# Cross-attention decoder layer: keys and values of all heads first, and projections as seven block products

## The chip, the cores and the metric

The kernel runs on one NeuronCore of a Trainium2 chip. A core has TensorE (PE: matmuls; its weight loads are listed as PEld), VectorE (DVE), ScalarE (ACT), GpSimd (POOL), SyncE (SP, which only issues DMAs here) and 16 DMA engines. The metric is device time of one execution in microseconds (us), lower is better. A time is the median of several runs.

## The reference

```python
x = x + attn(layernorm(x))                 # one head of 128, x is (8 batches, 128 tokens, 512), f32
x = x + xattn(layernorm(x), ctx, mask)     # 32 heads of 128, nearly all of the work
x = x + ffn(layernorm(x))                  # 512x512 base, plus top-2 of 8 low-rank experts

# xattn
xn = rmsnorm(h, ln_weight)
h_q, h_k, h_v = xn @ w_q.T, ctx @ w_k.T, ctx @ w_v.T        # each 1024 tokens x 4096
score = softmax(where(m, q k^T + position_bias, -inf))      # per batch and head, 128x128
out = h + (score @ v) @ w_out.T
```

Every f32 product of the projections is made of three fp32r passes: the operands are split in a high part (rounded to fp32r) and a low part (the rest), and hi*hi + hi*lo + lo*hi is accumulated. Scores and the weighing of values are plain f32 matmuls.

## The kernel before

**Tiling.** The 1024 tokens (8 batches of 128) are columns: `xt` (normalised x) and `ct` (context) are 512 features as 4 chunks `c` of 128 partitions x 1024 tokens, each as hi and lo. The 32 heads come in 16 groups of two (`PAIR`). Weights of a group arrive from DRAM as four pieces of 128x1024 (512 KB): QKA, QKB (query and key weights of head 0 and 1), WV, WO. ScalarE makes the high part (`split_weights`, L725), VectorE the low part from two SBUF tensors (`w_lo`, L1000).

**One group on PE**, in its order: `project_qk(g, 0)`, transpose of the last head's probabilities, scores of head 0, weighing of values, `project_v(g)`, transposes, `project_out(g - 1)`, `project_qk(g, 1)`, weighing, scores. `project_qk` makes, per head, two tensors (q and k) x two halves of 512 tokens x 4 chunks x 3 passes = 48 matmuls with 512 columns. `project_v` makes, per batch, 4 x 3 matmuls with 256 columns (both heads), 96 in a group. `project_out` makes, per batch, 2 heads x 3 passes with 512 columns, 48 in a group. PE is the engine whose order the others follow; every wait is written by hand, with semaphores.

**Around it.** VectorE adds bias and mask to the scores out of PSUM (`take_scores`, L960), takes maxima (L967), and after ScalarE's exponentials (L707) scales the probabilities by 1/sum (L973, `row_scale` L977, `probs` L981), splits outputs, and adds each batch's output product from PSUM to `acc` (`add_out`, L878). GpSimd does only `bias_mask` (L337, one 128x1024 addition a head) in the loop, and the low parts of `ct` at the start (L324) and of the FFN's weights at the end (L344). SyncE loads weights and bias.

**Start and end.** Ahead of the loop stand the one-head attention with its layernorms and group 0; the loop runs over groups 1 to 14, group 15 and the last output projection follow by hand, then the FFN. Group 1 begins at 96.2 us, and groups follow at 53.2 us.

Of the kernel before, what the change touches and what calls it, by code (L numbers as in the profile page):

```python
# [20 lines left out]
BANK = 512  # L35
NE, NR = 8, 16
ROUTED = 256
QKV_COLS, OUT_COLS = slice(0, KC * 3 * P), slice(KC * 3 * P, KC * 3 * P + C)
PIECE = PAIR * C
QKA, WV, WO, QKB = range(4)  # L40
# [5 lines left out]

def decoder_kernel(nc, x, ctx_t, mask, w_qkv, b_qkv, w_o, b_o, ln_w, pos_bias, weights, w_base, w_routed, w_lora_b,
                   out):
    with ExitStack() as ctx:
        def sb(name, shape, dt=F32):  # L50
            return ctx.enter_context(nc.sbuf_tensor(name, shape, dt))
# [3 lines left out]


        acc = sb("acc", [P, B, C])
        rows = sb("rows", [P, B, C])
        xt = [sb("xt_hi", [P, KC, T], F32R), sb("xt_lo", [P, KC, T], F32R)]
        ct = [sb("ct_hi", [P, KC, T], F32R), sb("ct_lo", [P, KC, T], F32R)]  # L60
        raw = sb("raw", [P, 4, PIECE])
        w = [sb("w_hi", [P, 4, PIECE], F32R), sb("w_lo", [P, 4, PIECE], F32R)]
        raw_a = sb("raw_a", [P, KC * 3 * P + C])

        ot = [sb("ot_hi", [P, PAIR * T], F32R), sb("ot_lo", [P, PAIR * T], F32R)]
        qt = sb("qt", [P, T])
        kt = sb("kt", [P, T])
        v = sb("v", [P, B, PAIR * P])
        probs = sb("probs", [P, B, P])
        probs_t = sb("probs_t", [P, B, P])  # L70
        bias = sb("bias", [P, PAIR, P])
        bias_mask = sb("bias_mask", [P, B, P])
        mask_add = sb("mask_add", [P, B, P])
        mask_raw = sb("mask_raw", [P, B, P], mask.dtype)
        has_key = sb("has_key", [P, B])
        b_o_rows = bias_mask[:, 0:C // P, :].rearrange("p b n -> p (b n)")
        b_qkv_cols = sb("b_qkv_cols", [P, 3])
        ln_w_cols = sb("ln_w_cols", [P, KC])
        ident = sb("ident", [P, P])
# [11 lines left out]
        neg_max = sb("neg_max", [P, B])  # L91
        sums = sb("sums", [P, B])
        inv = sb("inv", [P, B])
        row_scale = sb("row_scale", [P, B])
        logits = sb("logits", [P, B, NE])
        gates = sb("gates", [P, B, NE])

        beats, ties = (probs_t[:, n:n + 2, :].rearrange("p b (e j) -> p (b e) j", j=NE) for n in (0, 2))
# [5 lines left out]
        ot_last = [t[:, 0:PAIR, :].rearrange("p c n -> p (c n)") for t in xt]  # L104
        WO_LAST = QKA
        w_qkv_s = [t[:, QKV_COLS].rearrange("p (c n) -> p c n", c=KC) for t in ot]
        w_o_s = [t[:, OUT_COLS] for t in ot]
        vt_a = v[:, :, :].rearrange("p b n -> p (b n)")[:, 0:T]
        vt_tiles = v[:, :, :].rearrange("p b n -> p (b n)")[:, T:2 * T]
        ffn_cols = KC * C + KC * ROUTED + C  # L110
        ffn_raw = rows[:, :, :].rearrange("p b n -> p (b n)")[:, 0:ffn_cols]
        ffn = [t[:, :, :].rearrange("p c n -> p (c n)") for t in ct]
# [4 lines left out]

        bank = [ctx.enter_context(nc.psum_tensor(f"bank{i}", [P, BANK], F32)) for i in range(8)]
        QK, SC, TO, VO = bank[0:2], bank[2:4], bank[4:6], bank[6:8]
        ROWS_T = (SC + TO, SC + TO, TO + QK)  # L120
        OWN_OUT = (SC + QK) * 2
# [3 lines left out]

        x_loaded = [sem(f"x_loaded{b}") for b in range(B)]
        raw_loaded = [sem(f"raw_loaded{p}") for p in range(4)]
        raw_qkv_loaded = sem("raw_qkv_loaded")
        raw_o_loaded = sem("raw_o_loaded")
        small_loaded = sem("small_loaded")  # L130
        mask_loaded = sem("mask_loaded")
        bias_loaded = sem("bias_loaded")
        ffn_loaded = sem("ffn_loaded")
        stored = sem("stored")

        ident_ready = sem("ident_ready")
# [70 lines left out]
        def spans(layer, i):  # L207


            return 2 * layer + i + 2  # L210
# [140 lines left out]
        def _(pe):  # L351
# [148 lines left out]
            def last_out():  # L500
# [21 lines left out]
                for b in range(B):  # L522
# [6 lines left out]
                    if b >= 3:  # L529
                        part(b, 0)  # L530
# [752 lines left out]
```

## Time and profile before

| | us |
|---|---|
| median of 3 runs (965.95 to 966.62) | 966.17 |
| span of the profiled execution | 964.8 |
| PE busy | 937.4 (97%) |
| VectorE busy | 470.6 (49%) |
| ScalarE busy | 376.0 (39%) |
| GpSimd busy | 105.9 (11%) |
| DMA queue, share of 16 engines | 14.3% |

The profile shows one execution. A timeline row gives start, length and count of merged instructions; matmuls overlap, so what one costs is read from the distance of starts, not from its length. The chain of waits follows the last instruction back to what released it. PEclk is the granted TensorE clock as a share of 2.4 GHz.

### The profile page before, as it was taken

The page shows a single profiled execution, that of the slowest core. Times are in us where ns is not written, and L with a number is a line of the kernel's source. Part 1 is how long each engine was busy: PE and PEld are TensorE (multiplying, and loading weights), DVE is VectorE, ACT ScalarE, POOL GpSimd, SP SyncE. Part 2 cuts the span into 40 slices and gives each one's busy share as a digit, 9 for nine tenths or more (in the row PEclk, how much of TensorE's full clock was granted, in tenths as well). Part 3 has the DMA queues.
Part 4 walks back from the last instruction along what each step waited for, and adds up shares of the span by engine and source line. Part 5 has one row for each costly group of instructions (what it writes and reads, how often), then busy time and mean ns, then how long its engine had stood idle before and what let it go on. Part 6 is the DMA issues. An engine that isn't in the chain of part 4 may idle for free.

```text
span 964.8 us, 14659 instructions
## 1 busy us (share of the span) xinstructions
PE 937.4 (97%) x5584; PEld 831.5 (86%) x5584; DVE 470.6 (49%) x802; ACT 376.0 (39%) x999; POOL 105.9 (11%) x60
## 2 busy tenths in 40 slices
PE   4899999999999999999999999999999999999798
PEld 4788989889898989898898989898988989898587
DVE  7787545434444435444344444354443444444764
ACT  3555524343443515243434425252434344254030
POOL 3211101010000001010000000010100000000300
PEclk9999999999999999999999999999999999999899
DMA  6402120110111110101101111101011010200002
GB/s 239 131 1 72 50 66 27 42 45 27 46 47 43 32 61 27 65 27 32 55 27 43 49 43 29 64 27 65 24 28 62 27 43 27 98 1 1 0 1 88
DMA packets 15712, 45.45 MB, mean 47 GB/s; under 512 B 2000, under 2 KB 4176, under 8 KB 15568
## 3 DMA queue, kind: packets, MB, share of 16 engines
q1 hardware_dynamic: 15696, 45.23, 14.3%
q8 instruction: 11, 0.18, 0.1%
q14 instruction: 5, 0.04, 0.0%
HBM read 43.13 MB, written 2.10 MB: 47 GB/s over the span
## 4 chain that ended last, share of the span: by engine, by line
PE 93%; DVE 5%; DMA 1%; ACT 0%; POOL 0%; issue 0%; SPq 0%; DVEq 0%
PE bank L358 77%; PE bank L411 6%; PE bank L393 6%; PE bank L401 3%; DVE row_scale L977 1%; DVE rows L916 1%; DMA raw_a<-in_w_qkv 1%; PE bank L376 1%; DVE stats L886 0%; DVE acc L878 0%; DVE acc L1066 0%; DVE xt_lo L948 0%; DVE xt_lo L951 0%; DVE acc L1219 0%; POOL rstd L304 0%; ACT xt_hi L690 0%
## 5 line engine op out<-in xcount | busy, mean ns | idle before, releaser
L337 POOL TENSOR_TENSOR bias_mask<-mask_add,bias 128x1024 f32<-128x1024 f32 x32 | 76.7, 2395 | 713.2 <-DVE probs L960 702.7
L358 PE MATMUL bank<-w_hi,ct_hi 128*128 128x256 f32 x512 | 146.4, 286 | 0.0
L358 PE MATMUL bank<-w_hi,ct_lo 128*128 128x256 f32 x512 | 145.0, 283 | 0.0
L358 PE MATMUL bank<-w_lo,ct_hi 128*128 128x256 f32 x512 | 145.0, 283 | 0.0
L878 DVE TENSOR_TENSOR acc<-bank,acc 128x512 f32<-128x512 f32 x136 | 93.4, 691 | 78.6 <-PE bank L358 78.4
L725 ACT CAST w_hi<-raw 128x1024 fp32r<-128x1024 f32 x64 | 67.3, 1051 | 137.7 <-PE bank L358 137.7
L707 ACT ACTIVATE probs<-probs,neg_max 128x128 f32<-128x128 f32 x264 | 102.8, 393 | 43.1 <-DVE neg_max L967 43.1
L993 DVE TENSOR_TENSOR ot_lo<-bank,ot_hi 128x512 fp32r<-128x512 f32 x62 | 41.7, 689 | 136.8 <-ACT ot_hi L719 136.8
L1000 DVE TENSOR_TENSOR w_lo<-raw,w_hi 128x1024 fp32r<-128x1024 f32 x64 | 79.5, 1260 | 52.6 <-ACT w_hi L725 52.6
L358 PE MATMUL bank<-w_hi,ot_hi 128*128 128x512 f32 x240 | 95.8, 399 | 7.2 <-DVE acc L878 7.2
L358 PE MATMUL bank<-xt_hi,w_hi 128*128 128x512 f32 x256 | 101.6, 397 | 0.9 <-DVE xt_lo L948 0.7
L358 PE MATMUL bank<-ct_hi,w_hi 128*128 128x512 f32 x256 | 99.9, 390 | 0.4 <-DVE w_lo L1000 0.4
L358 PE MATMUL bank<-xt_lo,w_hi 128*128 128x512 f32 x256 | 99.8, 390 | 0.0
L358 PE MATMUL bank<-xt_hi,w_lo 128*128 128x512 f32 x256 | 99.8, 390 | 0.0
L358 PE MATMUL bank<-ct_hi,w_lo 128*128 128x512 f32 x256 | 99.8, 390 | 0.0
L358 PE MATMUL bank<-ct_lo,w_hi 128*128 128x512 f32 x256 | 99.7, 389 | 0.0
L358 PEld LDWEIGHTS bank<-w_hi,ct_hi 128*128 128x128 f32 x512 | 98.3, 192 | 0.3 <-ACT v L735 0.2
L358 PEld LDWEIGHTS bank<-w_lo,ct_hi 128*128 128x128 f32 x512 | 98.3, 192 | 0.1
L358 PEld LDWEIGHTS bank<-w_hi,ct_lo 128*128 128x128 f32 x512 | 98.2, 192 | 0.0
L358 PE MATMUL bank<-w_hi,ot_lo 128*128 128x512 f32 x240 | 94.2, 392 | 0.0
L358 PE MATMUL bank<-w_lo,ot_hi 128*128 128x512 f32 x240 | 94.0, 392 | 0.0
L731 ACT COPY kt<-bank 128x512 f32<-128x512 f32 x64 | 37.5, 586 | 118.8 <-PE bank L358 118.6
(133 smaller groups left out, 1505.0 us busy)
## 6 DMA issues: line engine op xcount, KB each, us to landing
raw<-in_weights SPq DMA_DIRECT2D x64, 512.0 KB, 3.5
acc<-in_x SPq DMA_DIRECT2D x8, 256.0 KB, 6.0
raw<-in_ctx_t SPq DMA_DIRECT2D x4, 512.0 KB, 8.2
bias<-in_pos_bias SPq DMA_DIRECT2D x16, 128.0 KB, 2.0
out_rows<-acc SPq DMA_DIRECT2D x8, 256.0 KB, 2.1
rows<-in_w_base SPq DMA_DIRECT2D x1, 1024.0 KB, 5.6
raw_a<-in_w_qkv SPq DMA_DIRECT2D x1, 768.0 KB, 6.9
rows<-in_w_routed SPq DMA_DIRECT2D x1, 512.0 KB, 6.4
```

Of the source, the lines that this page charges most:

```text
L337: pool.tensor_tensor(bias_mask[:, :, :], mask_add[:, :, :], bias[:, j, :].unsqueeze(1).to_broadcast([P, B, P]), ALU.add).then_inc(bias_mas ...
L358: ins = pe.matmul(out_ap, lhs[a], rhs[b], start=start and k == 0, stop=stop and k == n - 1)
L376: ins = pe.transpose(ROWS_T[layer][c][:, cols(t)], rows[:, HALF * i + t, cols(c)], ident[:, :])
L393: ins = pe.matmul(SC[i][:, cols(t)], qt[:, cols(b)], kt[:, cols(b)], start=True, stop=True)
L401: ins = pe.transpose(TO[i][:, cols(t)], probs[:, HALF * i + t, :], ident[:, :])
L411: ins = pe.matmul(TO[i][:, cols(t)], values(b), probs_t[:, b, :], start=True, stop=True)
L707: ins = act.activation(probs[:, b, :], probs[:, b, :], ACT.Exp, bias=neg_max[:, b:b + 1], accum_out=sums[:, b:b + 1])
L725: act.copy(w[0][:, piece if to is None else to, :], raw[:, piece, :]).then_inc(w_hi_ready[piece], 1)
L731: act.copy((qt, kt)[k // 2][:, cols(k % 2, BANK)], QK[k % 2][:, :]).then_inc(qk_copied, 1)
L878: dve.tensor_tensor(acc[:, b, :], of[:, :], acc[:, b, :], ALU.add).then_inc(out_added, 1)
L993: dve.tensor_tensor(to[1][:, c], TO[i][:, :], to[0][:, c].bitcast(F32), ALU.subtract).then_inc(ot_lo_ready, 1)
L1000: dve.tensor_tensor(w[1][:, to, :], raw[:, piece, :], w[0][:, to, :].bitcast(F32), ALU.subtract).then_inc(w_lo_ready[piece], 1)
```

## The change

1. **Two phases.** First keys and values of all 16 pairs of heads are projected and stored in DRAM (`keys`, `values`, 1 MB each a pair); then, pair by pair, queries are projected, keys and values loaded again, and attention and the output projection done. Everything of `project_qk`, `project_v` and the group order goes.
2. **Seven block products.** Each projection of a pair (two heads x 1024 tokens, 512 features) is seen as 2x2 blocks (heads x feature halves times feature halves x token halves) and made by the Strassen-Winograd scheme: 7 products (`project`, slots 0 to 6) of 2 chunks x 3 passes = 6 matmuls with 512 columns, 42 instead of 48. All run in two PSUM banks that accumulate in turn; ScalarE copies four partial results out (`take`), VectorE adds three.
3. **Sums of blocks.** For the weights, GpSimd makes four 128x256 sums (`sum_weights`), ScalarE four high parts (one of 256 and three of 512 columns), VectorE four low parts (`low`), for each of the three projections of a pair. Context and x get 4 sums, 7 high and 7 low parts of 128x1024, once: for the context on GpSimd, for x on VectorE, between pairs 1 and 3.
4. **Values.** They come out feature-major. VectorE transposes them in 32x32 blocks (`turn_blocks`, 4 operations of 128x512 a pair), and the DMAs put the blocks in place: the store writes runs of 32 floats (128 B), 8192 a pair in four DMAs; the load reads runs of 512 B.
5. **Attention phase.** The scaling of the probabilities moves from VectorE to GpSimd (`normalise_probs`), as does the low part of the output weights. The FFN's low parts are made after pair 0 and not at the end.

SyncE's order in the first phase (`ahead`): fetch key weights of the next pair, fetch its value weights, store keys, store values.

```diff
+            def store_keys(g):
+                sp.wait_ge(dve_took, 6 * g + 3)
+                sp.wait_ge(act_took, 8 * g + 4)
+                sp.dma_start(keys[g], st[0][:, :, :, :].rearrange("p i j n -> p (i j n)")).then_inc(k_stored, 16)
+
+            def store_values(g):
+                sp.wait_ge(v_turned, 4 * g + 4)
+                for d in range(4):
+                    sp.dma_start(values[g, :, :, :, d, :].rearrange("q b a n -> q (b a) n"),
+                                 turned[cols(d, QUAD), :, :, :, :].rearrange("q i b a n -> q (i b a) n")
+                                 ).then_inc(v_stored, 16)
+
...
+            def load_values(g):
+                for a in range(4):
+                    sp.dma_start(v[cols(a, QUAD), :, :, :].rearrange("q i b n -> q (i b) n"),
+                                 values[g, :, :, a, :, :].rearrange("q b d n -> q b (d n)")).then_inc(v_loaded, 16)
...
+            def sum_weights(p, m, free=None):
+
+                if free is not None:
+                    pool.wait_ge(product_done, free)
+                pool.wait_ge(raw_loaded[p], (p + 1) * 16 * (m + 1))
+                a11, a12, a21, a22 = (raw[p][:, n, :] for n in range(4))
+                s = w_sum[p]
+                pool.tensor_tensor(s[:, 1, :], a21, a22, ALU.add).then_inc(w_made[p], 1)
+                pool.tensor_tensor(s[:, 4, :], a11, a21, ALU.subtract).then_inc(w_made[p], 1)
+                pool.wait_ge(w_made[p], 4 * m + 1)
+                pool.tensor_tensor(s[:, 2, :], s[:, 1, :], a11, ALU.subtract).then_inc(w_made[p], 1)
+                pool.wait_ge(w_made[p], 4 * m + 3)
+                pool.tensor_tensor(s[:, 3, :], a12, s[:, 2, :], ALU.subtract).then_inc(w_made[p], 1)
+
...
+            def pair(g, last=False):
+                if not last:
+                    sum_weights(0, GROUPS + g + 1, SLOTS * (PAIRS_AHEAD + g + 1))
+                normalise_probs(g, 0)
+                if not last:
+                    add_mask(g + 1, 0)
+                normalise_probs(g, 1)
+                if not last:
+                    add_mask(g + 1, 1)
+                pool.wait_ge(wo_hi_ready, g + 1)
+                pool.tensor_tensor(wo[1][:, :, :].rearrange("p j n -> p (j n)"), raw_o,
+                                   wo[0][:, :, :].rearrange("p j n -> p (j n)").bitcast(F32),
+                                   ALU.subtract).then_inc(wo_lo_ready, 1)
+
...
+            def project(n, p, of, banks, slots=range(SLOTS), follow=None):
+
+                y, other = banks
...
+                                pe.wait_ge(act_took, 4 * n)
+                    elif s == 1:
+                        if not isinstance(n, int) or n:
+                            pe.wait_ge(act_took, 4 * n)
+                    elif s in (2, 3, 4):
+                        pe.wait_ge(act_took, 4 * n + s - 1)
+                    else:
+                        pe.wait_ge(dve_took, 3 * n + s - 4)
+                    if follow is not None:
+                        pe.wait_ge(follow, s + 1)
+                    to = (y, other, y, other, y, other, y)[s]
+                    three_pass(to[:, :],
+                               [([h[:, s, cols(k)] for h in w[p]], [h[:, s, k, :] for h in tok[of]])
+                                for k in range(2)], start=s in (0, 1, 5), again=True).then_inc(product_done, 1)
...
+            def pair(g, first=False):
+                project_queries(g, range(4))
+                if not first:
+                    turn_head_probs(g - 1, 1)
+                project_queries(g, range(4, SLOTS))
+
+                pe.wait_ge(dve_took, 3 * (PAIRS_AHEAD + g) + 3)
+                pe.wait_ge(k_loaded, 16 * g + 16)
+                head_scores(g, 0)
+                if not first:
+                    weigh_head_values(g - 1, 1)
+                pe.wait_ge(act_took, 4 * (PAIRS_AHEAD + g) + 4)
+                head_scores(g, 1)
+                if not first:
+                    project_out(g - 1, range(6))
+                turn_head_probs(g, 0)
+                if not first:
+                    project_out(g - 1, (6, 7))
+                weigh_head_values(g, 0)
+
...
+            def high_raw(p, m, free=None):
+
+                if free is not None:
+                    act.wait_ge(product_done, free)
+                act.wait_ge(raw_loaded[p], (p + 1) * 16 * (m + 1))
+                act.copy(w[p][0][:, A11_AT, :], raw[p][:, 0:1, :]).then_inc(w_hi_ready[p], 1)
+                act.copy(w[p][0][:, A_LAST, :], last_raw[p]).then_inc(w_hi_ready[p], 1)
+
+            def high_sums(p, m, which):
+
+                act.wait_ge(w_made[p], 4 * m + (3, 4)[which])
+                at = (S_C, S_D)[which]
+                act.copy(w[p][0][:, at, :], w_sum[p][:, at, :]).then_inc(w_hi_ready[p], 1)
+
...
+            def keys_pair(g, prepare=True):
+
+                act.wait_ge(k_stored, 16 * g)
+                if prepare:
+                    high_raw(1, g, 14 * g)
+                take(2 * g, 0, st[0], k_banks)
+                if prepare:
+                    high_sums(1, g, 0)
+                take(2 * g, 1, st[0], k_banks)
+                if prepare:
+                    high_sums(1, g, 1)
+                take(2 * g, 2, st[0], k_banks)
+                take(2 * g, 3, st[0], k_banks)
+
+            def values_pair(g):
+
+                high_raw(0, g + 1, 14 * g + 7)
+                if not isinstance(g, int) or g:
+                    act.wait_ge(v_turned, 4 * g)
+                take(2 * g + 1, 0, st[1], v_banks)
+                high_sums(0, g + 1, 0)
+                take(2 * g + 1, 1, st[1], v_banks)
+                high_sums(0, g + 1, 1)
+                take(2 * g + 1, 2, st[1], v_banks)
+                take(2 * g + 1, 3, st[1], v_banks)
...
+                dve.tensor_tensor(w[p][1][:, at, :], of, w[p][0][:, at, :].bitcast(F32),
+                                  ALU.subtract).then_inc(w_lo_ready[p], 1)
+
+            def take(n, which, to, banks):
+
+                y, other = banks
+                dve.wait_ge(product_done, SLOTS * n + which + 4)
+                dve.wait_ge(act_took, 4 * n + (3, 2, 1)[which])
+                i, j = ((0, 1), (1, 1), (0, 0))[which]
+                dve.tensor_tensor(to[:, i, j, :], (other, y, other)[which][:, :], to[:, i, j, :],
+                                  ALU.add).then_inc(dve_took, 1)
+
+            def turn_blocks(g, i, j):
+                dve.transpose(turned[:, i, half(j), :, :],
+                              st[1][:, i, j, :].rearrange("p (b a n) -> p b a n", a=4, n=QUAD)).then_inc(v_turned, 1)
...
+            def turn_pair(g):
+                if not isinstance(g, int) or g:
+                    dve.wait_ge(v_stored, 64 * g)
+                dve.wait_ge(dve_took, 6 * g + 6)
+                turn_blocks(g, 0, 0)
+                turn_blocks(g, 0, 1)
+                turn_blocks(g, 1, 1)
+                dve.wait_ge(act_took, 8 * g + 8)
+                turn_blocks(g, 1, 0)
+
...
+            def pair(g, first=False, last=False):
+                n = PAIRS_AHEAD + g
+                take(n, 0, qt, k_banks)
+                if not first:
+                    copy_probs_t(PAIR * g, probs_t)
+                take(n, 1, qt, k_banks)
+                take(n, 2, qt, k_banks)
+                for i in range(2):
+                    take_scores(g, 0, i)
+                for i in range(2):
+                    maxima(PAIR * g + 1, 0, probs[0], i)
+                if not first:
+                    split_head_out(g - 1, 1)
+                for i in range(2):
+                    take_scores(g, 1, i)
+                for i in range(2):
+                    maxima(PAIR * g + 2, 1, probs[1], i)
+                if not first:
+                    add_out(g, 0)
+                row_scales(g, 0, 0)
+                if not first:
+                    add_out(g, 1)
+                row_scales(g, 0, 1)
+                for b in range(2, 6):
+                    if not first:
+                        add_out(g, b)
+                    if not last and b < 4:
+                        low(0, GROUPS + g + 1, b - 2)
+                    if b >= 4:
+                        row_scales(g, 1, b - 4)
+                copy_probs_t(PAIR * g + 1, probs_t)
+                if not first:
+                    add_out(g, 6)
+                if not last:
+                    low(0, GROUPS + g + 1, 2)
+                if not first:
+                    add_out(g, 7)
+                if not last:
+                    low(0, GROUPS + g + 1, 3)
+                split_head_out(g, 0)
+
+            pair(0, first=True)
             with dve.Fori(1, GROUPS - 1) as g:
-                group(g)
-            group(GROUPS - 1, last=True)
-            copy_probs_t(HEADS)
-            split_out(HEADS, 1, to=ot_last)
+                pair(g)
+            pair(GROUPS - 1, last=True)
+            copy_probs_t(HEADS, probs_t)
+            split_head_out(GROUPS - 1, 1)
 
```

## Rows read from the trace of the kernel before

**Rows 1.** The page: busy time by engine, and the chain that ended last.
```profile
PE 937.4 (97%) x5584; PEld 831.5 (86%) x5584; DVE 470.6 (49%) x802; ACT 376.0 (39%) x999; POOL 105.9 (11%) x60
PE 93%; DVE 5%; DMA 1%; ACT 0%; POOL 0%; issue 0%; SPq 0%; DVEq 0%
```
**Rows 2.** PE's timeline inside group 5: start, length, instruction, shape, count.
```profile
309.26 0.39 PE L358 MATMUL bank<-xt_hi,w_lo 128*128 128x512 f32 x1
...
314.02 0.39 PE L358 MATMUL bank<-xt_hi,w_lo 128*128 128x512 f32 x1
...
319.69 1.03 PE L401 MATMUL bank<-ident,probs 128*128 128x128 f32 x8
320.56 2.02 PE L393 MATMUL bank<-kt,qt 128*128 128x128 f32 x16
322.42 1.95 PE L411 MATMUL bank<-probs_t,v 128*128 128x128 f32 x16
324.12 0.36 PE L358 MATMUL bank<-w_hi,ct_hi 128*128 128x256 f32 x1
324.33 0.28 PE L358 MATMUL bank<-w_lo,ct_hi 128*128 128x256 f32 x1
...
328.51 0.28 PE L358 MATMUL bank<-w_hi,ct_hi 128*128 128x256 f32 x1
```
**Rows 3.** GpSimd's timeline: its operations, with the idle time before them in brackets.
```profile
19.46 1.29 POOL L320 TENSOR_TENSOR ot_lo<-raw_a,ot_hi 128x512 fp32r<-128x512 f32 x1
20.72 5.03 POOL L324 TENSOR_TENSOR ct_lo<-raw,ct_hi 128x1024 fp32r<-128x1024 f32 x2
83.74 2.40 POOL L337 TENSOR_TENSOR bias_mask<-mask_add,bias 128x1024 f32<-128x1024 f32 x1 [3.15 <-DVE probs L960]
323.39 2.40 POOL L337 TENSOR_TENSOR bias_mask<-mask_add,bias 128x1024 f32<-128x1024 f32 x1 [11.19 <-DVE probs L960]
855.19 2.39 POOL L337 TENSOR_TENSOR bias_mask<-mask_add,bias 128x1024 f32<-128x1024 f32 x1 [11.21 <-DVE probs L960]
890.77 7.76 POOL L344 TENSOR_TENSOR ct_lo<-rows,ct_hi 128x3584 fp32r<-128x3584 f32 x1 [33.18 <-ACT ct_hi L772]
```
**Rows 4.** VectorE's timeline at the same moments (start, length, count).
```profile
19.53 6.96 DVE L916 TENSOR_SCALAR rows<-acc,mean_var,rstd 128x512 f32<-128x512 f32 x4 [1.12 <-POOL rstd L304]
49.85 2.69 DVE L878 TENSOR_TENSOR acc<-bank,acc 128x512 f32<-128x512 f32 x4
324.41 1.31 DVE L993 TENSOR_TENSOR ot_lo<-bank,ot_hi 128x512 fp32r<-128x512 f32 x2
890.85 7.70 DVE L977 TENSOR_TENSOR row_scale<-inv,has_key 128x4 f32<-128x4 f32 x1
```
**Rows 5.** One line's instructions each: w_lo (L1000), row_scale (L977); min/median/max ns.
```profile
L1000 DVE TENSOR_TENSOR w_lo<-raw,w_hi x64: 1215/1224/2462, 40.6 to 866.2; 128x1024 fp32r<-128x1024 f32 x64
L977 DVE TENSOR_TENSOR row_scale<-inv,has_key x64: 161/164/7699, 87.4 to 890.8; 128x4 f32<-128x4 f32 x64
```
**Rows 6.** Windows: length, busy us of PE, PEld, DVE, ACT, POOL, clock, DMA share, GB/s.
```profile
20.00:30.00 10.00, 5.59 (x28) 4.89 (x27) 8.09 (x7) 3.56 (x6) 5.75 (x3) 0.84 0.33 105
149.20:202.40 53.20, 53.20 (x323) 47.44 (x322) 23.35 (x39) 20.93 (x58) 4.79 (x2) 1.00 0.13 42
893.70:900.00 6.30, 0.07 (x1) 0.07 (x1) 6.27 (x4) 0.00 (x0) 4.83 (x1) 0.78 0.00 0
900.00:910.00 10.00, 10.00 (x47) 8.46 (x48) 4.76 (x8) 1.76 (x3) 0.00 (x0) 0.80 0.00 0
```
**Rows 7.** DMA over 379:381.5 (one bias load), then 10.2:11.8 (full load).
```profile
q1 hardware_dynamic: 144, 0.13, 17.2%
...
DMA packets 541, 0.60 MB, mean 377 GB/s; under 512 B 251, under 2 KB 251, under 8 KB 541
q1 hardware_dynamic: 541, 0.60, 106.7%
```
**Rows 8.** DMA issues: KB each, us from issue to landing.
```profile
bias<-in_pos_bias SPq DMA_DIRECT2D x16, 128.0 KB, 2.0
```

More of the change, by code:

```diff
@@ L53, in sem @@
         def sem(name):
             return ctx.enter_context(nc.semaphore(name))
+        KB = 1024
         acc = sb("acc", [P, B, C])
[L58 to L76, printed above, removed]
+        ctx_at, x_at = region(56 * KB), region(56 * KB)
@@ new lines, in _ @@
+            normalise(1, 1, (6, 7))
+            take_rows(0)
+            keys_pair(1)
+            take_rows(1)
+            values_pair(1)
+            keys_pair(2)
+            for n, slot in enumerate((0, 3, 5)):
+                x_high(slot)
+            act.wait_ge(x_made, 4)
+            x_high(1)
+            values_pair(2)
+            for slot in (2, 4, 6):
+                x_high(slot)
+            with act.Fori(3, GROUPS) as g:
+                keys_pair(g)
+                values_pair(g)
@@ new lines, in _, with split_last_rows @@
+            pair(0, first=True)
+            act.wait_ge(ffn_loaded, 48)
+            act.copy(ffn[0][:, :], ffn_raw[:, :]).then_inc(ffn_hi_ready, 1)
+            with act.Fori(1, GROUPS - 1) as g:
+                pair(g)
+            pair(GROUPS - 1, last=True)
+            copy_probs_t(HEADS, probs_t)
+            split_head_out(GROUPS - 1, 1)
+            normalise(2, 0, (0, 1))
+            def split_last_rows(i):
+                for c in range(KC):
+                    act.wait_ge(rows_t_done, 4 * KC + KC * i + c + 1)
+                    act.activation(xt[0][:, c, cols(i, BANK)], ROWS_T[2][c][:, :], ACT.Copy,
+                                   scale=1.0).then_inc(xt_hi_ready, 1)
@@ new lines, in take @@
+            def take(n, which, to, banks):
+                y, other = banks
+                dve.wait_ge(product_done, SLOTS * n + which + 4)
[6 more added lines that the diff above has]
+                              st[1][:, i, j, :].rearrange("p (b a n) -> p b a n", a=4, n=QUAD)).then_inc(v_turned, 1)
@@ new lines, in values_pair @@
+            def values_pair(g):
+                for part in range(4):
+                    low(0, g + 1, part)
+                for which in range(3):
+                    take(2 * g + 1, which, st[1], v_banks)
+            def turn_pair(g):
+                if not isinstance(g, int) or g:
+                    dve.wait_ge(v_stored, 64 * g)
[5 more added lines that the diff above has]
+                turn_blocks(g, 1, 0)
@@ L1105, in _ @@
+            keys_pair(2)
+            values_pair(2)
+            turn_pair(2)
+            for slot in HIGH:
+                x_low(slot)
             dve.wait_ge(mask_loaded, 16)
```

989 lines of the change are left out of this document (533 added, 456 removed).

## The prediction

> **What bounds the kernel now.** I read the page first: PE is busy 97% of the span, and the chain that ended last runs through PE for 93% [rows 1]. In the windows, one whole group (149.2 to 202.4) has PE busy for 53.20 of 53.20 us, VectorE for 23.4, ScalarE for 20.9, GpSimd for 4.8, and the granted clock is 1.00 [rows 6]. GpSimd's bias additions at the same place of groups 5 and 15 are 531.8 us apart, so a group is 53.18 us [rows 3]. PE's timeline says of what it is made: 21 matmuls with 512 columns take 314.02 - 309.26, 0.227 us each; 35 with 256 columns take 328.51 - 324.33, 0.119 each; a head costs 0.87 for its transposes, 1.86 for its scores and 1.70 for its values [rows 2]. 144 x 0.227 + 96 x 0.119 + 2 x 4.4 is 52.9, so PE never waits there. The exception is the end: from 893.7 to 900 PE works 0.07 us [rows 6], because VectorE's tiny row_scale took 7.70 us [rows 4] while GpSimd's FFN split ran for 7.76 [rows 3]. The span is 964.8; medians lie 1.4 us above it, which I add at the end.
>
> **What PE saves.** Queries and keys of a pair go from 96 to 84 matmuls: 12 x 0.227 = 2.72 us. Values go from 96 x 0.119 = 11.4 to 42 x 0.227 = 9.53: 1.9 us. 16 pairs x 4.65 = **-74 us**. A first-phase pair is then 84 x 0.227 = 19.05 us of PE, an attention pair 9.53 (queries) + 10.9 (output) + 8.9 (heads) = 29.3 to 30. The other engines' totals fit below both, so what matters is order.
>
> **Lock between VectorE and GpSimd.** Row_scale's 7.70 us instead of 0.164 [rows 5], w_lo's 2462 ns instead of 1224 [rows 5] next to a bias addition (83.74 [rows 3]), and four normalisations that took 6.96 us at 19.53 [rows 4] next to 5.03 us of GpSimd [rows 3] say: a VectorE operation whose inputs are both in SBUF (or a fast SBUF-to-SBUF one) waits until GpSimd's current operation ends, and GpSimd's next one lets it in. Operations with one input in PSUM don't: ot_lo at 324.41 keeps its pace [rows 4] beside a bias addition. The change moves GpSimd from 4.8 us a group to about 15 of 30: four sums of 256 columns (0.73 each, on the line through 1.29 us for 512 and 2.40 for 1024 [rows 3]), four scalings of 1.29, two bias additions and one split of 2.40. Beside them VectorE has eight operations with two SBUF inputs: `row_scales` and `low`. I follow its order from the end of the scores (15.7 us into the pair), VectorE at 0.6 us an operation (four additions start within 2.69 - 0.69 us [rows 4]). `row_scales(g,0,1)` and the first `low` wait some 0.7 each for a scaling, the second `low` 1.8 for the first bias addition, `row_scales(g,1,1)` 0.7, and the last `low` 1.8 for the second bias addition. These 5.7 us stand ahead of the last four `add_out`, which free PE's banks (PE waits 0.8), and of the last `low`, on which the next pair's queries wait: it ends near 32.4 instead of 30. Above 29.4: 3.0 us x 15 pairs = **+45 us**. Bounds: 1 us a pair (the orders miss each other, +15) to 5 (+75). In the first phase the locked operations are 0.73 long and meet slack of 0.5 to 1 us ahead of slots 2 to 6: nothing.
>
> **Values to DRAM.** No store of 128 B runs is in the trace. Its price per packet is bounded by rows 7: below by the tiny packets (the full window has 541 packets in 1.067 x 16 x 1.6 = 27.3 us of engine time; its 290 of 2 KB, at the window's 377 / 16 = 23.6 GB/s an engine, are 25.2 of them, which leaves 2.1 us for 251 tiny ones, 8 ns each), above by a 1 KB packet (0.172 x 16 x 2.5 us / 128 = 54 ns). I take 14 ns, near the tiny row, since 128 bytes add 5 to its 8: 8192 / 16 x 14 ns = 7.2 us a pair (4 to 28). What stands behind it is the fetch of the next key weights, on the same queue. The turned blocks are complete some 2 us into the next pair, the first packet flies about 1 us later (a bias load lands after 2.0 us, of which 128 / 16 packets are 0.4 [rows 7, 8]), so weights land at 2.9 + 7.2 + 1.4 (256 packets of 2 KB) + 0.2 = 11.7 us. They are wanted at 10.1, when ScalarE ends the keys' last copy. ScalarE's high parts stand ahead of its first `take` of the values, and PE's slot 2 waits for that at 12.3, slot 3 for the second, behind GpSimd's third sum: 2 us late in all. 14 pairs x 2.0 = **+28 us** (0 at 10 ns, about 310 at 54 ns, each further ns costing 0.5 us a pair). VectorE's four transposes have no row: between 0.54 (a fast SBUF operation) and 1.3 us each; I take 0.69, and even 1.3 only delays the store by 2.4. The Vector Engine (DVE) Microarchitecture Reference of the Trainium skill, section 3.8, has the transposing front-end sustain one element per cycle and lane; no run here shows it, and the sum stands without it.
>
> **Edges.** Start: the first product needs context sums that GpSimd makes in 2.4 us pieces (4 sums and 7 splits, 26 us, before 4 x 2.4), with the own attention's locked VectorE operations between them and the last three high parts behind ScalarE's second exponentials; the own attention and the first two products end about 7 us later than the same work now: **+7** (3 to 15). VectorE's x sums (4 x 1.22) and low parts (7 x 1.22, mask 1.9) stand ahead of the `low` and `take` of pairs 2 and 3, where there are 4 us of slack: **+14** (5 to 18). First attention pair: keys land some 3 us after the queries are done, and softmax has no output projection to hide under (25 us for 15.6 of work), then a 3.2 us ScalarE split of FFN weights: **+12** (8 to 16). Idle stretches drop the clock to 0.78 to 0.84 for about 10 us [rows 6]; this is inside these margins. End: the 7.7 us lock goes with the split, most of the 6.3 idle and 2 of low clock: **-8** (-6 to -10). Loads in the second phase (keys, values in 512 B runs, about 9 us of DMA in 30) hide.
>
> **Sum.** 964.8 - 74 + 45 + 28 + 7 + 14 + 12 - 8 = 988.8, plus 1.4: **990 us**, slower by 2.5%.
>
> **Rivals.** *It works as meant.* Stores at 10 ns or less hide, bias additions fall where VectorE waits for PE anyway (1 us a pair), edges at their low ends: 964.8 - 74 + 15 + 0 + 3 + 5 + 8 - 10 + 1.4 = 913, up to 960 with two of the terms at my values. For it: PE is the only full engine and its work falls by 8%; against it: 7.70 us at 890.85. *Small writes are dear.* The DMA queue becomes the bound of the first phase at 25 to 54 ns a packet: 5.5 to 20 us a pair more than my 2, so 1070 to 1280. For it: a run of 128 B is far below all that this kernel moves in bulk; against it: the tiny packets' 8 ns. DMA: Bandwidth & Descriptors of the Trainium skill, Specifications, asks for at least 512 B and has the engine read, modify and write below that; by that rule this rival would hold, and no row here has such a write. *The products are not fewer or not as fast:* 42 matmuls at 0.227 follow from the code and from rows 2; under 2 in 100.
>
> **Chances.** My forecast (960 to 1040) 0.45, of which a few hundredths fall within 0.2% of before, about what a measurement of this kernel can tell from no change; as meant (below 964) 0.33; dear writes (above 1040) 0.22. Faster 0.34, same 0.04, slower 0.62. The range takes a tenth off each end: 925 to 1095; the forecast's own is 960 to 1030.
>
> **What would show it.** A first-phase pair's period: 19.1 right for the first rival, 21 for me, above 25 for dear writes, with ScalarE's w_hi waiting for DMA. An attention pair's period: 32.4 against 30, with VectorE `w_lo` and `row_scale` rows far over their 0.6 and 0.16 us. The store's packets: 128 B, 14 ns. FFN split: no long row_scale at the end. I am wrong if GpSimd and VectorE interleave without waits, or if the stores are in nobody's way.

## The result, and the profile after

Before 966.39 us (median of 4 runs), after **1084.68 us** (1081.75 to 1089.31, 4 runs): ratio 1.123, 95% interval 1.120 to 1.126. I had forecast 990, range 925 to 1095. The time lies inside the range, near its end; the direction held and the size did not: 12.3% slower, not 2.5%. The profiled execution is the slowest of the four (1089.31). Its span is 1087.6 us, 98.8 above the 988.8 of my sum, and of these some 5 are the distance of this run from the median.

The page of the changed kernel: busy time, the clock in 40 slices, the chain that ended last (by engine, then by line).

```profile
PE 929.8 (85%) x4528; PEld 771.6 (71%) x4528; DVE 693.9 (64%) x1077; ACT 420.4 (39%) x1089; POOL 384.5 (35%) x339
...
PEclk9898888999899999988989998999899989998999
...
PE 60%; DVE 19%; issue 9%; POOL 5%; DMA 3%; ACT 2%; SPq 2%; DVEq 0%; POOLq 0%; ACTq 0%
PE bank L541 49%; DVE w_lo L1189 10%; PE bank L595 5%; DVE acc L1070 3%; PE bank L613 3%; DMA raw<-in_weights 2%; PE bank L605 1%; POOL w_sum L438 1%; POOL ctx_lo L455 1%; PE bank L559 1%; SPq L318 1%; POOL w_sum L435 1%; DVE stats L1077 1%
```

Beside [rows 1]: PE was busy 97% of the span and is now busy 85%. By my sum its work fell by 74 us, yet its busy time fell by 7.6 (937.4 to 929.8). The clock line says why: 13 of the 40 slices are below 0.9. The mean granted clock is 0.928 (0.995 before), and with the two levels 1.00 and 0.50 that is some 157 us of the span at the lower one (10 before). PE was busy for 121 us of these (8 before), and half of that, 60 us, would not be there at full clock. A fifth of the chain is VectorE's, and `w_lo` alone, the low parts of the weights, is a tenth.

The windows show where the span lies: start, pairs 1 and 2 with the x work, the rest of the first phase, attention pair 0, attention pairs 1 to 15, the end (columns as in [rows 6]).

```profile
0.00:96.00 96.00, 61.52 (x270) 49.71 (x271) 72.79 (x126) 37.90 (x71) 49.51 (x46) 0.88 0.30 96
96.00:162.20 66.20, 50.53 (x210) 40.20 (x208) 43.17 (x55) 28.49 (x49) 14.24 (x14) 0.89 0.50 116
162.20:456.40 294.20, 261.57 (x1073) 207.60 (x1074) 162.61 (x230) 105.67 (x204) 83.63 (x105) 0.95 0.56 134
456.40:494.80 38.40, 19.78 (x99) 16.32 (x99) 18.73 (x28) 13.07 (x44) 12.17 (x10) 0.80 0.65 175
494.80:1021.00 526.20, 477.40 (x2553) 406.58 (x2551) 359.41 (x552) 223.71 (x702) 220.50 (x162) 0.93 0.32 90
1021.00:1087.60 66.60, 59.01 (x331) 51.22 (x329) 37.22 (x89) 11.53 (x21) 4.43 (x5) 0.97 0.09 32
```

**Attention pairs.** GpSimd's first weight sums of the pairs at 543.29 and 966.28 are twelve pairs apart: 35.25 us a pair, where I had 32.4. The end of one pair on GpSimd, VectorE (its two scale operations and its second to fourth `low`, the operations named `w_lo`) and PE:

```profile
876.93 2.38 POOL L489 TENSOR_TENSOR bias_mask<-mask_add,bias 128x1024 f32<-128x1024 f32 x1
879.25 2.81 POOL L519 TENSOR_TENSOR wo_lo<-raw,wo_hi 128x1024 fp32r<-128x1024 f32 x1
...
869.26 0.35 DVE L1163 TENSOR_TENSOR row_scale<-inv,has_key 128x4 f32<-128x4 f32 x1
...
871.96 1.87 DVE L1189 TENSOR_TENSOR w_lo<-raw,w_hi 128x512 fp32r<-128x512 f32 x1
...
875.46 0.40 DVE L1163 TENSOR_TENSOR row_scale<-inv,has_key 128x4 f32<-128x4 f32 x1
...
876.97 2.88 DVE L1189 TENSOR_TENSOR w_lo<-w_sum,w_hi 128x512 fp32r<-128x512 f32 x1
...
880.38 2.23 DVE L1189 TENSOR_TENSOR w_lo<-w_sum,w_hi 128x512 fp32r<-128x512 f32 x1
...
882.83 0.79 PE L541 MATMUL bank<-x_hi,w_hi 128*128 128x512 f32 x1 [3.40 <-DVE w_lo L1189]
883.42 0.63 PE L541 MATMUL bank<-x_lo,w_hi 128*128 128x512 f32 x1
...
888.97 0.40 PE L541 MATMUL bank<-x_hi,w_lo 128*128 128x512 f32 x1
```

The third `low` waits out the bias addition (876.93 to 879.31), the fourth starts inside `wo_lo`, GpSimd's low part of the output weights, and ends just after it; each takes 0.69 us undisturbed. PE idles for 3.4 us. Then 14 matmuls start some 0.43 us apart (883.42 to 888.97) and not 0.227. Windows over the same pair, up to the idleness, behind it, and after that:

```profile
860.50:882.80 22.30, 18.93 (x119) 16.51 (x117) 20.56 (x32) 12.33 (x43) 14.61 (x11) 0.98 0.37 94
882.80:888.60 5.80, 5.77 (x14) 4.52 (x15) 1.00 (x2) 0.83 (x2) 0.00 (x0) 0.50 0.66 203
889.00:896.50 7.50, 7.50 (x40) 6.26 (x39) 2.77 (x4) 1.23 (x3) 0.00 (x0) 1.00 0.00 0
```

0.50 is the lower level, 1.2 GHz. In pairs of 34.8 to 34.9 us the stretch is 8 to 11 matmuls long, in those of 36.1 us 14. Over the 14 waits of this kind, the slow matmuls cost 1.2 to 2.6 us each time by distance of starts, 1.9 on average.

**First phase.** From 206.38 to 433.64 ten pairs pass, 22.7 us each, where I had 21.05. In one of them SyncE's queue, GpSimd's first sum of the next key weights, and PE show:

```profile
230.12 4.60 SPq L318 DMA_DIRECT2D values<-turned  x4
235.28 1.22 SPq L289 DMA_DIRECT2D raw<-in_weights  x1
...
240.63 0.73 POOL L435 TENSOR_TENSOR w_sum<-raw 128x256 f32<-128x256 f32 x1 [9.32 <-DMA raw<-in_weights]
...
242.05 0.50 PE L541 MATMUL bank<-ctx_hi,w_hi 128*128 128x512 f32 x1 [1.70 <-ACT st L915]
...
244.56 0.50 PE L541 MATMUL bank<-ctx_hi,w_hi 128*128 128x512 f32 x1 [0.86 <-ACT st L915]
```

The starts of PE's matmuls are 2.1 and 1.2 us apart here, where 0.23 would do. ScalarE's copies come late because its high parts of the late weights stand ahead of them. Six of the ten pairs take about 22.1 us at full clock; the others take 23.0 to 25.2 at a mean clock of 0.86 to 0.93.

### The profile page after: what moved, and what is told of

It is laid out like the page before. It is cut to its first block, busy times and chain, and to the rows that moved or that the text cites. A ratio compares the mean times of both kernels' runs of the same rounds, so it can differ in the third digit from the quotient of the medians.

```text
span 1087.6 us, 14912 instructions
## 1 busy us (share of the span) xinstructions
PE 929.8 (85%) x4528; PEld 771.6 (71%) x4528; DVE 693.9 (64%) x1077; ACT 420.4 (39%) x1089; POOL 384.5 (35%) x339
## 4 chain that ended last, share of the span: by engine, by line
PE 60%; DVE 19%; issue 9%; POOL 5%; DMA 3%; ACT 2%; SPq 2%; DVEq 0%; POOLq 0%; ACTq 0%
PE bank L541 49%; DVE w_lo L1189 10%; PE bank L595 5%; DVE acc L1070 3%; PE bank L613 3%; DMA raw<-in_weights 2%; PE bank L605 1%; POOL w_sum L438 1%; POOL ctx_lo L455 1%; PE bank L559 1%; SPq L318 1%; POOL w_sum L435 1%; DVE stats L1077 1%; DVE probs_t L1168 1%; ACT st L915 1%
## 5 line engine op out<-in xcount | busy, mean ns | idle before, releaser
L915 ACT COPY st<-bank 128x512 f32<-128x512 f32 x192 | 112.5, 586 | 357.6 <-PE bank L541 355.9
L541 PE MATMUL bank<-ctx_hi,w_hi 128*128 128x512 f32 x448 | 187.3, 418 | 65.0 <-ACT st L915 57.8
L1198 DVE TENSOR_TENSOR st<-bank,st 128x512 f32<-128x512 f32 x144 | 99.5, 692 | 203.0 <-PE bank L541 202.9
L541 PE MATMUL bank<-ctx_lo,w_hi 128*128 128x512 f32 x448 | 182.4, 407 | 0.0
L541 PE MATMUL bank<-ctx_hi,w_lo 128*128 128x512 f32 x448 | 181.7, 405 | 0.0
L541 PEld LDWEIGHTS bank<-ctx_hi,w_hi 128*128 128x128 f32 x448 | 88.6, 198 | 97.4 <-ACT st L915 71.1
L541 PE MATMUL bank<-x_hi,w_hi 128*128 128x512 f32 x224 | 103.8, 464 | 49.6 <-DVE w_lo L1189 48.8
L1189 DVE TENSOR_TENSOR w_lo<-w_sum,w_hi 128x512 fp32r<-128x512 f32 x96 | 119.5, 1258 | 29.4 <-POOL w_sum L440 25.1
L541 PE MATMUL bank<-wo_hi,ot_hi 128*128 128x512 f32 x256 | 104.5, 408 | 1.8 <-POOL wo_lo L519 1.8
L541 PE MATMUL bank<-wo_lo,ot_hi 128*128 128x512 f32 x256 | 100.0, 391 | 0.0
L541 PE MATMUL bank<-wo_hi,ot_lo 128*128 128x512 f32 x256 | 100.0, 390 | 0.0
```

The source lines that it names most:

```text
L541: ins = pe.matmul(out_ap, lhs[a], rhs[b], start=start and k == 0, stop=stop and k == n - 1, skip_group_check=again)
L915: act.copy(to[:, i, j, :], (y, other, y, y)[which][:, :]).then_inc(act_took, 1)
L1189: dve.tensor_tensor(w[p][1][:, at, :], of, w[p][0][:, at, :].bitcast(F32), ALU.subtract).then_inc(w_lo_ready[p], 1)
L1198: dve.tensor_tensor(to[:, i, j, :], (other, y, other)[which][:, :], to[:, i, j, :], ALU.add).then_inc(dve_took, 1)
```

## Experiments

Experiments 1 to 5 and 11 are medians of two runs, which lie 1 to 7 us apart; 6 to 10 of four to ten. The kernel before, run beside each batch, took 965.4 to 966.9 us (medians). Experiments 1 to 5 each make one edit to the changed kernel; from 6 on they build on earlier ones.

**1. SyncE's order alone.**

```diff
-            def ahead(g, last=False):
-                sp.wait_ge(w_lo_ready[0], 4 * g + 4)
...
-                    fetch_heads(g + 1, K_COLS)
+            def ahead(g, heads=K_COLS):
                 sp.wait_ge(w_lo_ready[1], 4 * g + 4)
...
                     fetch_values(g + 1)
                 store_keys(g)
+                if heads is not None:
+                    sp.wait_ge(w_lo_ready[0], 4 * g + 8)
+                    fetch_heads(0 if heads == Q_COLS else g + 2, heads)
                 store_values(g)
```

> SyncE's order alone: the fetch of the next pair's key weights is issued ahead of the store of the values, as soon as the weights before it are used up. In the changed kernel a pair of the first phase takes 22.7 us on average against 19.05 us of PE work, and PE waits 2.1 and 1.2 us in it for the banks that ScalarE frees late, because ScalarE's high parts stand ahead of them and wait for these weights. Theory (the weights land late because they stand behind the store): both waits go, a pair takes 19.1 to 19.5, 13 pairs save 3.3 each: 43 us less, about 1041. Rival (the DMA engines are short of time, whatever the order; they are busy 0.61 of a pair): the value weights or the key store come late instead, a pair stays above 21.5 and the time above 1065.

Measured **1042.3**, 42 us less. GpSimd's sums follow every 9.52 us, 19.04 a pair, which is PE's own work:

```profile
344.78 0.74 POOL L436 TENSOR_TENSOR w_sum<-raw 128x256 f32<-128x256 f32 x1 [6.49 <-PE bank L542]
...
363.82 0.74 POOL L436 TENSOR_TENSOR w_sum<-raw 128x256 f32<-128x256 f32 x1 [6.48 <-PE bank L542]
```

The store flies as before, and costs nothing here once the key weights don't stand behind it. The DMA engines were not short of time.

**2. Long runs, same place in the queue.**

```diff
                 for d in range(4):
-                    sp.dma_start(values[g, :, :, :, d, :].rearrange("q b a n -> q (b a) n"),
-                                 turned[cols(d, QUAD), :, :, :, :].rearrange("q i b a n -> q (i b a) n")
+                    sp.dma_start(values[g, cols(d, 8), :, :, :, :].rearrange("q b a d n -> (q b a d n)")
+                                 .rearrange("(p n) -> p n", p=QUAD),
+                                 turned[cols(d, QUAD), :, :, :, :].rearrange("q i b a n -> q (i b a n)")
                                  ).then_inc(v_stored, 16)
```

> The values are stored in runs of 8 KB and not of 128 B, in the same four DMAs at the same place of the queue; left out is that the blocks come to their places in DRAM, so the attention weighs shuffled values. In the changed kernel the store's packets fly for 6.5 us at 200 GB/s, and SyncE needs 4.6 us to issue its four DMAs and 1.2 for the weights behind. If the packets' price is what delays the weights: the store takes 2.8 us (1 MB at 377 GB/s), the weights land some 3.5 us earlier, a pair takes 19.1 to 19.6, about 1042. If SyncE's issuing is what delays them: they land only 1 us earlier, a pair takes 21.5 to 22, about 1070.

Measured **1064.2**, between the two. The kernel leaves out that the blocks of the values come to their places, so its attention weighs shuffled values. A pair takes 20.79 us; the weights come 11.0 us into it and not 12.4:

```profile
226.75 2.71 SPq L318 DMA_DIRECT2D values<-turned  x4
230.01 0.64 SPq L289 DMA_DIRECT2D raw<-in_weights  x1
...
235.87 0.74 POOL L436 TENSOR_TENSOR w_sum<-raw 128x256 f32<-128x256 f32 x1 [7.93 <-DMA raw<-in_weights]
```

So neither account alone: with long runs SyncE issues the four stores in 2.7 us and not 4.6, a gain that I had not foreseen, and the fetch still needs 5.8 us from its issue behind 1 MB of store. The length of the runs is about half of what a pair loses (1.9 of 3.7 us), the place in the queue all of it. This run doesn't part the flight of the packets from their issue: it shortens both.

**3. VectorE's order alone.**

```diff
+                    if not last and b >= 4:
+                        low(0, GROUPS + g + 1, b - 2)
                     if b >= 4:
                         row_scales(g, 1, b - 4)
...
-                    low(0, GROUPS + g + 1, 2)
...
-                    low(0, GROUPS + g + 1, 3)
```

> Attention phase, VectorE's order alone: the last two low parts of the next query weights stand behind add_out 4 and 5 and not behind add_out 6 and 7, so ahead of GpSimd's second bias addition and its split of the output weights. In the changed kernel a pair takes 35.25 us: 29.4 of work, 3.4 that PE waits for the last low part (which starts only when GpSimd's wo_lo is nearly done) and 2.8 in which the next 14 matmuls run at half the granted clock. Theory (lock and, as its consequence, the clock): both go, a pair takes 29.4 to 30.2, 14 pairs save 5 to 5.8: 75 us less, about 1010. Rival (the clock falls in this phase by itself, for all engines' load): the wait goes, the slow matmuls stay: 32, about 1040. Rival (the row scales, now 1.3 us later, delay add_out and the bias addition): 31 to 34 with PE waiting elsewhere.

Measured **1000.3**, 84 us less. One whole pair of this kernel:

```profile
728.50:758.10 29.60, 29.60 (x174) 25.50 (x172) 21.02 (x37) 14.85 (x48) 14.23 (x12) 1.00 0.40 111
```

No idle time, full clock, with GpSimd's amount of work unchanged. This phase's load does not lower the clock.

**4. The wait filled.** 15 matmuls of 512 columns stand ahead of each pair's queries, so that PE works where it waited.

```diff
+                if not first:
+                    pe.wait_ge(dve_took, 3 * (PAIRS_AHEAD + g))
+                    pe.wait_ge(act_took, 4 * (PAIRS_AHEAD + g))
+                    for k in range(15):
+                        pe.matmul(QK[0][:, :], tok[OF_X][0][:, 0, 0, cols(0)], tok[OF_X][0][:, 0, 0, :],
+                                  start=True, stop=True, skip_group_check=True)
                 project_queries(g, range(4))
```

> Ahead of each pair's queries in the attention phase (15 pairs) PE makes 15 more matmuls of 512 columns into the bank that the first product overwrites; their result is used by nobody. At full clock they take 3.4 us and fill the time in which PE waits for the last low part. Theory (the half clock of the next 14 matmuls is a consequence of the 3.7 us of idleness): they run at 0.227 and not 0.427 us, a pair takes 32.4 to 32.8 and not 35.25, 15 pairs save 2.6 each: 40 us less, about 1045, though nothing was taken away. Rival (the clock falls for another reason, or the wait was shorter than the filling): 35.2 or more, 1085 to 1090.

Measured **1054.2**: more work, 30 us less. Where the filling stands (722.8 to 726.2), and then the queries:

```profile
722.80:726.20 3.40, 3.40 (x18) 2.74 (x16) 3.40 (x3) 0.71 (x2) 2.98 (x2) 1.00 0.00 0
726.20:731.90 5.70, 5.70 (x26) 4.57 (x25) 1.33 (x3) 1.77 (x3) 0.00 (x0) 1.00 0.60 207
```

A pair takes 33.1 us (PE weighs values at 721.12 and again at 754.23), which is experiment 3's 29.6 and the 3.4 of filling; I had expected 32.4 to 32.8. The clock stays at 1.00 and the queries' matmuls at their pace. The mean granted clocks say the same of the whole: 0.961 here and 0.959 in experiment 3 are each some 82 us at the lower level, where the changed kernel has 157. The half clock is a consequence of the idleness.

**5. `wo_lo` later.** GpSimd splits the output weights during the next pair's queries.

```diff
             def pair(g, last=False):
+                if not isinstance(g, int) or g:
+                    pool.wait_ge(product_done, SLOTS * (PAIRS_AHEAD + g) + 2)
+                    out_low(g - 1)
                 if not last:
...
+                if last:
+                    out_low(g)
+
+            def out_low(g):
                 pool.wait_ge(wo_hi_ready, g + 1)
```

> The changed kernel with one edit: GpSimd's split of the output weights (wo_lo) is made 30 us later, while the next pair's queries are being projected, and not behind the second bias addition. VectorE's order is as in the changed kernel. There the last low part starts when wo_lo is nearly done. Theory (VectorE's operation on two SBUF inputs waits for the end of GpSimd's current one, and slips in between two): the third low part still waits for the bias addition, the last one follows it at once: PE waits 1.5 to 2 us and not 3.7, an attention pair takes 32 to 33.5 with less half clock, 1035 to 1055. Rival (the low parts are only slowed by GpSimd's traffic, or the fetch of output weights behind wo_lo lands late and takes the place): 34.5 or more, above 1070.

Measured **1049.0**. VectorE's last two low parts, and GpSimd:

```profile
747.65 2.87 DVE L1196 TENSOR_TENSOR w_lo<-w_sum,w_hi 128x512 fp32r<-128x512 f32 x1
...
751.05 0.68 DVE L1196 TENSOR_TENSOR w_lo<-w_sum,w_hi 128x512 fp32r<-128x512 f32 x1
...
747.61 2.37 POOL L489 TENSOR_TENSOR bias_mask<-mask_add,bias 128x1024 f32<-128x1024 f32 x1
756.27 2.39 POOL L526 TENSOR_TENSOR wo_lo<-raw,wo_hi 128x1024 fp32r<-128x1024 f32 x1 [6.29 <-PE bank L548]
```

The third still waits for the bias addition, the last has nothing to wait for and takes 0.68. PE's waits of the same place, thirteen pairs apart:

```profile
525.16 0.49 PE L548 MATMUL bank<-x_hi,w_hi 128*128 128x512 f32 x1 [1.90 <-DVE w_lo L1196]
...
946.88 0.49 PE L548 MATMUL bank<-x_hi,w_hi 128*128 128x512 f32 x1 [1.89 <-DVE w_lo L1196]
```

A pair takes 32.4 us on average. PE waits 1.9 (2.1 with the slower start of the first matmul) in every pair. Behind 7 of the 14 waits 10 or 11 matmuls run at the lower level, and such a pair takes 33.3; the others take 31.7. This is the lock step by step: one operation of GpSimd, one wait.

**6. Both orders (1 and 3).**

> Both orders together: SyncE fetches key weights ahead of the store, VectorE's last two low parts stand behind add_out 4 and 5. Alone they took 42 us (1042.3) and 84 us (1000.3) off the changed kernel's 1084.7. They concern different phases, so theory: they add, 958, faster than the kernel before by 0.9%; a first-phase pair takes 19.05, an attention pair 29.6. Rival (part of what one took away was the other's, or the same warm clock): 965 to 975.

Measured **963.5** against 965.4 before, ratio 0.998 (0.997 to 1.000): the gains nearly add (958 expected), and the changed kernel with both orders is level with the one before.

**7 and 8. GpSimd's order at the start; then the low parts of x in threes.** In the changed kernel PE waits longest at two places, both behind ScalarE, which waits for GpSimd's sums:

```profile
82.67 0.79 PE L541 MATMUL bank<-ctx_hi,w_hi 128*128 128x512 f32 x1 [10.35 <-ACT st L915]
...
165.95 0.79 PE L541 MATMUL bank<-ctx_hi,w_hi 128*128 128x512 f32 x1 [11.31 <-ACT st L915]
```

```diff
             sum_weights(1, 0)
+            sum_weights(0, 1, 7)
             root(1, half(0), spans(1, 0))
...
             ahead(2)
+            with pool.Fori(3, GROUPS) as g:
+                ahead(g)
             pool.wait_ge(mask_ready, 1)
             add_mask(0, 0)
             add_mask(0, 1)
-            with pool.Fori(3, GROUPS) as g:
-                ahead(g)
```

> As the last one, and GpSimd's order at the start: the four sums for the key weights of pair 1 go ahead of the root operations of the layernorm (in the changed kernel they start at 79.4 because GpSimd waits for VectorE's statistics, and PE waits 10.7 us for a bank behind ScalarE's high parts of them); the two bias additions of pair 0 go behind the first phase (in the changed kernel they wait for VectorE's mask from 137 to 157.5 and take 4.8, ahead of pair 3's sums; PE waits 12.0 us). Theory (GpSimd's order): the first wait goes, of the second 5 to 8 us, and 2 to 4 us of half clock behind them: 940. Rival (VectorE's own x work, 8.0 us of low parts and 5.6 of sums, sets these waits): 952 or more.

> As the last one, and VectorE's seven low parts of x, 8.0 us in one piece ahead of pair 3's work, are spread: three behind pair 2's transposes, three behind pair 3's, one and the mask behind pair 4's. Theory: three of them (3.4 us) fit between the transposes and the first take of a pair (there are 4 us), so that the rest of pair 3's wait goes: 5 to 8 us below the last one. Rival (VectorE was not late there any more): within 1 us of it.

Measured **959.1** (0.993) and **960.8** (0.995). I expected 940 and some 933: both missed. In the first (GpSimd's order), half of each wait stays, now named after VectorE, and a new one of 3.5 us comes at 403.6. In the second (the low parts of x, three at a time) the rest of pair 3's wait is gone, and two others stand in pairs 4 and 5:

```profile
177.02 0.50 PE L543 MATMUL bank<-ctx_hi,w_hi 128*128 128x512 f32 x1 [2.17 <-DVE st L1200]
...
199.99 0.50 PE L543 MATMUL bank<-ctx_hi,w_hi 128*128 128x512 f32 x1 [1.95 <-DVE st L1200]
```

Three operations, 3.9 to 4.3 us together, are more than the place between the transposes and the next pair's low parts has room for.

**9. The x work in single pieces** at each half pair, the second half of the layernorm's statistics and the turning of x later, pair 0's bias additions in pairs 7 and 8.

> As b3_edges, with the work around the first pairs spread: the second half of the layernorm's statistics behind pair 0's values, x turned one product later, x sums two and two behind the key copies of pairs 2 and 3, high and low parts of x one at each half pair from 2 to 5, the bias additions of pair 0 in pairs 7 and 8. In b3_edges PE waits 5.8, 4.2, 3.7, 3.4, 2.5 and 5.2 us between 75 and 160 us, and 3.5 at 403. Theory (each is one engine's queue that a burst of x work delays; in pieces of 1.2 us it fits into the slack): 15 to 25 us less with the half clock behind the waits, 935 to 945. Rival (the slack is not there at these places, as spreading in threes only moved the wait to pairs 4 and 5 and took nothing off): 952 or more.

Measured **935.0**, ratio 0.967 (0.965 to 0.969), 24 us below experiment 7. Of the waits between 75 and 160 us five of 1.0 to 2.1 us are left. Several things were moved at once, so what each is worth stays open.

**10. Pair 1's query weights ahead of the last store** of values, on experiment 9's kernel.

> As b6_polish, but SyncE fetches pair 1's query weights ahead of the last store of values, as soon as pair 0's are used up, and not behind the first keys and values and the three FFN loads. In b6_polish, as in the changed kernel, ScalarE waits 13.3 us for these weights in pair 0 of the attention phase, its exponentials of pair 0 stand behind that, and PE waits 9.9 us for the first scaled probabilities. Theory (a queue again: the first pair is long because the weights of the second are late): exponentials start 6 us earlier, PE's wait falls to 3 to 5, 5 to 8 us in all, 927 to 930. Rival (the softmax has nothing to hide under, so that the wait is the softmax itself): within 2 us of b6_polish, 933 to 935.

Measured **928.8**, ratio 0.962 (0.960 to 0.963), 3.9% faster than the kernel before. The first scaled probabilities reach PE after 3.7 us and not 9.9 (in brackets the part that counts as idle), first experiment 9's kernel, then this one:

```profile
411.97 1.09 PE L611 MATMUL bank<-ident,probs 128*128 128x128 f32 x4 [9.61 <-POOL probs L511]
```

```profile
406.32 1.09 PE L614 MATMUL bank<-ident,probs 128*128 128x128 f32 x4 [3.46 <-POOL probs L514]
```

**11. The saved products given back,** on experiment 7's kernel: product 5 is made twice.

> As b3_edges, but each of the 48 projections makes product 5 twice (the first result is overwritten), so 48 matmuls and not 42: what the block products save on queries and keys is given back. Theory (with the two orders mended PE is the bound in both phases): 48 x 6 x 0.227 = 65 us more than b3_edges. Rival (something else ends last in one of the phases): less, 20 to 45.

Measured **1019.5**, 60.4 more. A first-phase pair takes 21.8 us and not 19.05, an attention pair 30.9 and not 29.6: PE bounds both phases, and the matmuls saved are worth what I took for them, 18 in three projections of a pair.

## Why the prediction was wrong in size

**What PE saves, -74: right.** Experiment 11 priced a matmul saved (60 us for the 65 that 288 of them should cost), and the periods of 19.04 and 29.6 in experiments 1 and 3 are my 19.05 and 29.3 to 30. Together they are 48.6 us a pair against 53.2 before, 73 us in 16 pairs.

**Lock, +45: mechanism right, size wrong by 43.** That the next queries wait for the last `low` was forecast, and 3.0 us a pair above the work; measured 3.4, which is 6 us in 15 pairs, and 0.2 of more work. I had the last `low` wait for the second bias addition. That is what the third waits for; the last waits for `wo_lo` (experiment 5), which my walk through the order left out. That the wait came out near its forecast is in part luck: VectorE's operations on two SBUF inputs lose 0.2, 0.0, 1.2, 0.2, 2.2 and 1.5 us in the pair shown, 5.3 in all where I had 5.7, but I had put 0.7 on each of three small ones and nothing on the third `low`. The step that failed is "Idle stretches drop the clock ... this is inside these margins": I had [rows 6] with 0.78 to 0.84 behind idleness, kept it for the edges, and priced a wait that comes in every pair at its own length. What the half clock behind it costs is on average 35.25 - 29.6 - 3.4 = 2.2 us, or 33 in 15 pairs (1.9 by distance of starts; the difference is that a wait costs some 0.3 more than its length in brackets), and experiment 4 gave 30 of them back by filling the wait. The bounds of 1 to 5 us a pair had no term for what follows a wait.

**Values to DRAM, +28: mechanism right, some 20 short.** The 13 pairs of the third window take 294.2 us, 20.6 more than 13 x 21.05. A packet of 128 B was priced at 14 ns. It costs 10: in 2 us of the store (232 to 234) 3147 / 16 packets fly.

```profile
DMA packets 3147, 0.40 MB, mean 200 GB/s; under 512 B 3147, under 2 KB 3147, under 8 KB 3147
```

The whole store, with a dip, flies from 231.5 to 237.2, 11 ns a packet. By my line "0 at 10 ns" next to nothing would have been lost. But SyncE takes 4.6 us to issue the four DMAs, so that the fetch is issued 7 us into the pair and lands 5.3 us later: at 12.4, where I had 11.7. I had priced the packets and not the issuing, and the weights' own flight behind the store at 1.6 us, where it took 3.4. Which of the two weighs more stays open. PE then loses 3.1 us a pair at full clock and not 2.0, and 3.7 on average with the half clock that four of the ten pairs have. "DMA: Bandwidth & Descriptors" of the Trainium skill, Specifications, asks for at least 512 B to reach the line's rate. In that the trace agrees: 200 GB/s against the 377 of [rows 7]. My rival took it for a bound of the whole phase, and that it is not: with the same packets a pair takes PE's own time in experiment 1.

**Start +7, x +14, first pair +12, end -8.** What is left of the 98.8 is about 36 us (98.8 - 15 x 2.85 - 20.6), and lies here. Attention pair 0 takes 38.4 us for 15.6 of work: PE's starts show 21.7 us of waiting, 10 above my term. I held the softmax to be the reason; experiment 10 shows 6 us of it to be the weights of pair 1, which stand in SyncE's queue behind 1.8 MB of FFN weights and in ScalarE's ahead of the exponentials. The end gives 71.1 - 66.6 = 4.5 and not 8. The long `row_scale` is gone, as forecast (the longest of this kernel takes 2.1 us), but PE waits 2.1 us for the last `wo_lo`; the rest stays open. Up to pair 3 that leaves some 43 us where I had 21: PE's waits between 72 and 166 are 36 of them (10.7, 4.0, 3.7, 3.1, 2.5, 12.0), and the rest goes with the half clock (0.88 and 0.89 in the first two windows). My step saw VectorE's x work and "4 us of slack"; it did not follow GpSimd's queue, where the layernorm's roots and pair 0's bias additions stand ahead of weight sums, nor the chain from there over ScalarE's high parts to its copies. Experiment 7 bears that out for half of the two longest waits; the other half is named after VectorE. That the first phase's locked operations cost nothing is not contradicted: with the fetch in time a pair takes PE's own time.

**Rivals.** *As meant* (913 to 960, 0.33) was not what the change did, yet 928.8 lies inside it: the same computation with other orders. *Small writes are dear* (above 1040, 0.22) names the right size for the wrong reason. *The products are not fewer* fell with experiment 11.

## What to carry to other kernels

A wait of TensorE that recurs is priced at its length plus the slow matmuls behind it, here 1.2 to 2.6 us after 3.4 of idleness, so that moving two VectorE operations up by a few us was worth 84. When a change adds work to the helping engines, follow each in-order queue from the new work to TensorE, DMA issue time included: the same operations in other orders ran in 1085 and in 929 us. Lay added work out singly, where each engine has room for one piece: in threes it only moved the wait (experiment 8), in single pieces, with other moves beside it, it went under (experiment 9).

## What the runs showed of the hardware that I had not expected

- Waits of 3.4 us of an otherwise full TensorE were followed by 8 to 14 matmuls of 512 columns at 1.2 GHz (0.427 us each). Of the 14 waits of 1.9 us in experiment 5's kernel 7 were followed by 10 or 11 such matmuls, the others by none. In the first phase the six pairs whose longer wait was 1.4 to 1.7 us had none; the four with 2.0 to 2.4 had 6 to 13.
- Issuing a DMA of 256 KB took SyncE 1.15 us in runs of 128 B and 0.68 in runs of 8 KB.
- Writes in runs of 128 B flew at 200 GB/s over 16 engines, 10 ns a packet and engine.
- One `low` of VectorE (0.69 us undisturbed) took 2.88 us beside GpSimd's bias addition of 2.38, and the next one (2.23) waited in the same way for the GpSimd operation that followed.
- VectorE's 32x32 transposes of 128x512 took 2.49 us for four, 0.62 each: the fast end of my bounds.
